# A transformer layer with routed experts: the expert weights are split during attention, rows go to DRAM in long pieces

## The reference, cut to what matters

```
x = layernorm(x + attention(x))
logits = x @ Wg.T;  w, idx = top_k(softmax(logits), 2);  w = w / w.sum()
h = silu(x @ W1[e].T) * (x @ W3[e].T)          # HIDDEN = 352
y = sum over the two experts of w * (h @ W2[e].T)
x = layernorm(x + y)
```

## Time and profile before

| | us |
|---|---|
| three timed runs | 981.38, 982.62, 983.60 (median 982.62) |
| profiled execution, its time | 989.87 |
| its span in the trace | 988.1 |
| attention ends, routing starts | 455.5 |
| routing: VectorE ends | 499.24 |
| experts' stage: first instruction | 499.51 |
| TensorE busy over the span | 799.6 (81%) |
| VectorE, ScalarE, GpSimd busy | 585.2, 480.5, 552.4 |

### The profile page before, as it was taken

How to read it: one execution, slowest core, us unless ns; L and a number is a source line. 1 busy time by engine, 2 the same in 40 slices (tenths; PEclk the granted TensorE clock), 3 DMA queues, 4 the chain that set the end, 5 groups by cost and what they waited for, 6 DMA issues and landing times. The chain is left out here.

```text
span 988.1 us, 22538 instructions
## 1 busy us (share of the span) xinstructions
PE 799.6 (81%) x7657; PEld 598.8 (61%) x7658; DVE 585.2 (59%) x1478; ACT 480.5 (49%) x1150; POOL 552.4 (56%) x719
## 2 busy tenths in 40 slices
PE   5899999999999999982538877888777778787866
PEld 3556666666666666551228776877767777686722
DVE  4678888888888888827935433434434343343445
ACT  1377777777777777755713222222223222222347
POOL 6146666666666666654054666656665656666543
PEclk9899999999999999975668988898998898999979
DMA  5334444434434443204921111111111111112178
GB/s 168 103 122 134 135 135 134 132 131 129 127 127 136 135 135 129 75 8 176 163 46 30 44 41 44 41 41 42 44 43 39 43 42 43 43 42 43 36 238 280
DMA packets 71596, 93.98 MB, mean 95 GB/s; under 512 B 10336, under 2 KB 50016, under 8 KB 71232
## 3 DMA queue, kind: packets, MB, share of 16 engines
q1 hardware_dynamic: 62640, 74.21, 24.1%
q0 software_dynamic: 8704, 17.98, 7.0%
q10 hardware_dynamic: 144, 0.35, 0.1%
HBM read 56.26 MB, written 34.14 MB: 91 GB/s over the span
## 5 line engine op out<-in xcount | busy, mean ns | idle before, releaser
L377 DVE TENSOR_REDUCE neg_max<-ps_s 128x6 f32<-128x768 f32 x256 | 241.1, 952 | 38.7 <-PE ps_s L564 32.7
L242 POOL TENSOR_SCALAR_AFFINE_SELECT probs<-probs 128x512 f32<-128x512 f32 x256 | 162.4, 634 | 164.7 <-ACT probs L314 159.1
L314 ACT ACTIVATE probs<-ps_st 128x768 f32<-128x768 f32 x256 | 207.5, 811 | 81.5 <-PE ps_st L578 80.9
L1122 ACT ACTIVATE act_a<-ps_a 128x352 f32<-128x352 f32 x136 | 63.5, 467 | 310.7 <-DMA dense<-shift_t 160.4
L1103 POOL DMA_INDIRECT picked_rows<-rows_out,pairs x136 | 134.0, 986 | 134.1 <-ACT rows_out L1126 109.9
L1096 POOL DMA_INDIRECT xg<-x_rows,pairs x136 | 131.6, 968 | 79.8 <-issue 40.5
L1160 DVE TENSOR_TENSOR x_low<-ps_xy,x_high 128x128 fp32r<-128x128 f32 x136 | 39.1, 287 | 216.6 <-ACT x_high L1130 173.6
L558 PE MATMUL ps_s<-dense 32*128 32x256 f32 (+1 forms) x1024 | 117.9, 306 | 19.1 <-ACT probs L314 9.3
L1231 PE MATMUL ps_xy<-w_sb,h_t 128*128 (+1 forms) x816 | 129.2, 300 | 1.7 <-ACT rows_out L1126 1.7
L558 PEld LDWEIGHTS ps_s<-dense 32*128 32x128 f32 x1024 | 82.2, 191 | 78.2 <-issue 46.7
L1231 PEld LDWEIGHTS ps_xy<-w_sb,h_t 128*128 128x128 f32 (+1 forms) x816 | 120.6, 213 | 7.1 <-issue 6.8
(11 more groups left out here) (181 smaller groups left out, 1390.6 us busy)
## 6 DMA issues: line engine op xcount, KB each, us to landing
dense_rows<-split SPq DMA_DIRECT2D x32, 512.0 KB, 2.7
dense<-dense_rows SPq DMA_DIRECT2D x64, 256.0 KB
dense<-dense_rows SPq DMA_DIRECT2D x64, 128.0 KB
pick<-picked_rows SPq DMA_DIRECT2D x16, 512.0 KB, 6.0
x_rows<-y_all SPq DMA_DIRECT2D x8, 520.0 KB, 8.1
xt_sb<-xt SPq DMA_DIRECT2D x32, 128.0 KB, 2.2
x_sb<-x SPq DMA_DIRECT2D x32, 128.0 KB, 2.4
out<-normal SPq DMA_DIRECT2D x16, 256.0 KB
```

The source lines that it names most:

```text
L242: last = pool.affine_select(out=part, in_=part, compare_op=ALU.is_ge, fill=0.0, base=0, pattern=[[0, 2 * BLOCKS], [1, P]], channel_multipl ...
L314: act.activation(probs[:, g, 2 * half:2 * half + 2, 0:L + P], ps_st[:, :, 0:L + P], ACT.Exp, scale=float(HEAD_DIM) ** -0.5).then_inc(exp_d ...
L377: v.tensor_reduce(out=neg_max[:, h * GROUP + j:h * GROUP + j + 2, :], in_=ps_s[:, j:j + 2, 0:L + P].rearrange("p b (c t) -> p b c t", t=P) ...
```

## The change

1. Splitting the weights moves from routing into attention. w1 and w3 are taken in 16 pieces of 128x352 (one expert's matrix each) through a ring of four buffers. Four pieces are loaded ahead of the loop and split in the first iteration behind g = 3; one piece is split in each of the batches 0 to 11, behind the work of g = 0. ScalarE copies a piece rounded, VectorE waits for that and subtracts. SyncE loads a later piece at the end of each iteration and w2 in three loads at the end of batches 16 to 18.
2. The DRAM row of token (tile t, place p) becomes p * 64 + t, so that each of the 128 partitions stores eight tiles as one piece of 8 * 520 = 4160 bytes instead of eight pieces of 520. The gathered addresses are computed accordingly (`at_row`), which makes `token` unnecessary.
3. The experts of the 136 tiles are found with two comparisons and a sum over 8 columns on VectorE and two products with the identity on TensorE, instead of a comparison and a reduction over 128x1088.
4. The share block moves to ahead of `place_i`.

```
         for b in range(FIRST, LAST):                                 # ScalarE, attention
...
+                    for c in pieces_at(b, g):
+                        act.wait_ge(piece_landed[c % PIECE_RING], 16 * (c // PIECE_RING + 1))
+                        act.activation(kept["w_high"][:, piece_columns(c)], piece[:, c % PIECE_RING, :], ACT.Copy).then_inc(
+                            piece_high, 1)
...
+                    for c in pieces_at(b, g):                        # VectorE, attention
+                        dve.wait_ge(piece_high, c + 1)
+                        v.tensor_tensor(kept["w_low"][:, piece_columns(c)], piece[:, c % PIECE_RING, :],
+                                        kept["w_high"][:, piece_columns(c)].bitcast(F32), ALU.subtract).then_inc(
+                            piece_low, 1)
...
+        def pieces_at(b, g):
+            if b == FIRST:
+                return range(PIECE_RING) if g == GROUPS - 1 else ()
+            return (b + PIECE_RING,) if g == 0 and 0 <= b < PIECES - PIECE_RING else ()
...
+            def load_piece(c):                                       # SyncE
+                if c >= PIECE_RING:
+                    sp.wait_ge(piece_low, c - PIECE_RING + 1)
+                sp.dma_start(piece[:, c % PIECE_RING, :], (w1, w3)[c // E][:, piece_columns(c % E)]).then_inc(
+                    piece_landed[c % PIECE_RING], 16)
+            for c in range(PIECE_RING):
+                load_piece(c)
...
+                if b == -1:
+                    for c in range(PIECE_RING, 2 * PIECE_RING):
+                        load_piece(c)
+                if 0 <= b < PIECES - 2 * PIECE_RING:
+                    load_piece(b + 2 * PIECE_RING)
+                if W2_AT <= b < W2_AT + len(W2_PARTS):
...
+                    sp.dma_start(kept["w2"][0:m, i * E * D:(i + 1) * E * D], w2[c:c + m, :]).then_inc(w2_landed, 16)
...
-            rows = x1_rows.rearrange("(c t p) d -> c p t d", p=P, t=STORE)
+            rows = x1_rows.rearrange("(p t) d -> p t d", p=P)
...
-                sp.dma_start(rows[c], y_all[:, c * STORE:(c + 1) * STORE, :]).then_inc(x1_stored, 16)
+                sp.dma_start(rows[:, at, :], y_all[:, at, :]).then_inc(x1_stored, 16)
...
+            for i, first in enumerate(sides_at):
+                last = v.tensor_scalar(passed[:, i, :], ends[:], -float(first), consts_at("partition"), ALU.add, ALU.is_le)
+            chain(last)
+            v.tensor_reduce(out=passed_sum[:], in_=passed[:], axis=AX.X, op=ALU.add).then_inc(passed_ready, 1)
...
-            for i in range(2):
-                dve.wait_ge(high_done, i + 1)
-                part = slice(i * WIDE, (i + 1) * WIDE)
-                v.tensor_tensor(w_low[:, part], w_raw[:, part], w_high[:, part].bitcast(F32), ALU.subtract)
-                take(turns - 2 + i)
-            chain(v.tensor_tensor(
-                ge_end[:], consts_at("iota")[:, 0:places].rearrange("p (i o) -> p i o", o=1).to_broadcast([P, places, E]),
-                ends[:].rearrange("p (o e) -> p o e", o=1).to_broadcast([P, places, E]), ALU.is_ge))
-            chain(v.tensor_reduce(out=expert_f[:], in_=ge_end[:], axis=AX.X, op=ALU.add))
-            v.tensor_scalar(expert_of[:], expert_f[:], E - 1.0, None, ALU.min)
+            take(turns - 2)
+            take(turns - 1)
+            dve.wait_ge(experts_listed, 1)
+            v.tensor_scalar(expert_of[0:1, :], ps_total[0:1, 0:places], E - 1.0, None, ALU.min)
...
+                last = mm(ps_total[0:1, first:first + wide], passed_sum[:, i:i + 1], consts_at("ident")[:, 0:wide],
+                          start=True, stop=True)
```

More of the change, by code:

```diff
@@ L47, in attention @@
     FIRST, LAST = -3, n + 2
+    PIECES, PIECE_RING = 2 * E, 4
+    W2_PARTS = range(0, HIDDEN, P)
+    W2_AT = 16
     CHOSEN = 8
@@ L67, in attention @@
         averages = sb("averages", [P, P])
+        piece = sb("piece", [P, PIECE_RING, HIDDEN])
         bias_logits = sb("bias_logits", [P, E])
@@ L124, in attention @@
             sem, ("xb_ready", "y_ready", "stats_ready", "mv_ready", "y_kept"))
+        piece_landed = [sem(f"piece_landed{i}") for i in range(PIECE_RING)]
+        piece_high, piece_low, w2_landed = map(sem, ("piece_high", "piece_low", "w2_landed"))
         CHOICE_STEPS = 9
@@ L656, in _, with routing @@
                     router()
-def routing(nc, consts_at, w1, w3, w2, kept, x1_rows):
+def routing(nc, consts_at, kept, x1_rows):
     y_all, mv_all, choice = kept["y"], kept["mv"], kept["choice"]
@@ L711, in routing @@
         numbers_at, tiles_at = (sb(k, [P, turns, P], BF16) for k in ("numbers_at", "tiles_at"))
-        ge_end = sb("ge_end", [P, places, E])
-        expert_f = sb("expert_f", [P, places])
         second = kept["second"]
[L715 to L719, removed]
+        found, inside, empty, at_row, row = (
+            sb(k, [P, places]) for k in ("found", "inside", "empty", "at_row", "row"))
+        sides_at = range(0, places, P)
+        passed = sb("passed", [P, len(sides_at), E])
+        passed_sum = sb("passed_sum", [P, len(sides_at)])
         ps_behind = ctx.enter_context(nc.psum_tensor("ps_behind", [P, 512], F32))
@@ L928, in _ @@
             chain(v.scalar_tensor_tensor(inside[:], second[:], -float(P), found[:], ALU.mult, ALU.add))
-            chain(v.scalar_tensor_tensor(token[:], ps_keys[:, turns:turns + places], float(P), inside[:], ALU.mult,
-                                         ALU.add))
-            v.tensor_scalar(pairs[:, :, 0], token[:], -1.0, 0.0, ALU.add, ALU.max)
             chain(v.scalar_tensor_tensor(at_row[:], inside[:], float(tiles), ps_keys[:, turns:turns + places], ALU.mult,
                                          ALU.add))
+            v.tensor_scalar(pairs[:, :, 0], at_row[:], -float(tiles), 0.0, ALU.add, ALU.max)
             chain(v.scalar_tensor_tensor(row[:], second[:], float(tokens), at_row[:], ALU.mult, ALU.add))
@@ L951, in _ @@
                    ones[0:1, 0:1], start=True, stop=True).then_inc(keys_turned, 1)
+            pe.wait_ge(passed_ready, 1)
+            for i, first in enumerate(sides_at):
+                wide = min(P, places - first)
+                last = mm(ps_total[0:1, first:first + wide], passed_sum[:, i:i + 1], consts_at("ident")[:, 0:wide],
+                          start=True, stop=True)
+            last.then_inc(experts_listed, 1)
             def spread_out(c):
@@ L1284, in build @@
             "pairs": sb("pairs", [P, places, 2], I32), "expert_of": sb("expert_of", [P, places], I32),
-        }
[L1286 to L1290, removed]
+            "w_high": sb("w_high", [P, 2 * EXPERTS * HIDDEN], F32R),
+            "w_low": sb("w_low", [P, 2 * EXPERTS * HIDDEN], F32R),
+            "w2": sb("w2_sb", [P, -(-HIDDEN // P) * EXPERTS * D]),
+        }
+        attention(nc, x, xt, wqkv, bqk, bv_columns, wo, wo_rows, bo, bo_columns, wg, cst, consts, w1, w3, w2,
+                  kept, dense_rows)
+        routing(nc, consts_at, kept, x1_rows)
         experts_and_combine(nc, consts_at("ident"), consts_at("eps"), kept, x1_rows, picked_rows, out)
```

43 lines of the change are left out of this document (19 added, 24 removed).

## The result

In the first comparison (5 executions of each kernel, in turns) the changed kernel took a median of 978.11 us against 982.62, a ratio of 0.9963, 95% interval 0.9945 to 0.9981: 4.5 us faster. By far the larger part of the measurements says that the change makes no difference that can be told, as the likeliest case of the prediction had it (982.5 against 982.62 before). The first ratio was not seen again, and why it came out so stays open.

The account below looks back on a forecast made before the run. The prediction took TensorE to bound attention and VectorE the routing stage. Its terms, +5.2 + 0.4 - 5.7 = -0.1 us, gave a median of 982.5 us against 982.62, own range 980 to 985.

Parts of the forecast that it names:

- the likeliest case: Whole kernel: the routing stage's gain is paid back in attention; 982.5 us, own range 980 to 985, chance 0.50.
- (b): Attention: the split is hidden because the pipeline takes up 0.43 us a batch; 977.3 us, chance 0.16.
- (f): Experts' stage: it changes by itself, most likely by one 4.9 us wait; 977.6 or 987.4 us, chance 0.10.
- The copies in attention: Attention, 12 batches: a ScalarE copy before the exponential releasing TensorE costs 0.43 us each, +5.2 (4.4 to 5.8).
- VectorE's subtraction: Attention, behind the second row maximum: 0.5 us long, cost put at 0; without cover up to 1.0 us a batch.
- The lead-in: Before the first scores: four piece loads and their split delay router() from 9.07 to 11.5; +0.4 us (0 to 3).
- (d): Lead-in: pieces land later than 10.5 and router() holds the first scores; 985.5 us with 3 us late, chance 0.06.
- Routing: Routing stage: VectorE's chain shortens, the last store sets the end at 493.5; 5.7 us earlier (3.7 to 6.2).
- (e): Routing stage: large pieces don't speed the store, the last lands in 4.7 us, gain 3.7; 984.5 us, chance 0.08.
- The sum: Whole kernel: attention +5.2, lead-in +0.4 and routing -5.7 make -0.1 us; profiled 989.8, median 982.5.
- The experts' stage: Tile loop from 500 us on: only gathered row addresses change, gathers are issued 12 tiles ahead; 0 us.
- My own sign of being wrong: Attention and experts' stage: wrong if the copy takes well under 0.37 us or the experts' stage moves over 3 us.

Follow-up runs that it names:

- the two further ratios: The changed kernel timed again against the kernel before in two further series, no edit: ratios 1.0013 and 0.9996.

## Why the prediction was right, and where its terms were off

The likeliest case held: the routing's gain is paid back in attention and the lead-in. The first comparison's 978.11 alone would not have said so: it lies outside the forecast's own 980 to 985, next to the 977.3 and 977.6 of rivals (b) and (f). What bears the forecast out is the two further ratios and the stages of the traces. By its steps:

- **The copies in attention, +5.2 forecast.** The place and the mechanism were right: the period grew to 12.99 (13.0 forecast), only in the batches with a piece, and moving the copy alone behind that exponential, on top of the subtraction, took all of it back. Rival (b), that it is hidden, is refuted. The mis-sized term is the copy: 0.38, where I took 0.43 from 0.37 to 0.48. The line from the 128-column to the 2816-column copy gave 0.57 as its duration, its row says 0.50; the bound from below, a 352-column row less the queue's overlap, was nearly exact. Eleven periods of 0.385 make 4.2; the twelfth copy, in batch 0, shows no cost (14.6 to 14.7 us to the next copies, 14.5 to 14.8 in the kernel before).
- **VectorE's subtraction, 0.** Right: its row says 0.53 (0.5 forecast), and the maxima behind it run late without holding TensorE; with it at the end of the batch the period did not change.
- **The lead-in, +0.4 forecast.** Wrong in size. The third batch's copies start at 27.34, 26.73 and 27.24 in three profiles with the changed lead-in, and at 25.57, 25.46 and 25.31 with the old one, 1.65 us later on average. Two steps failed. I let the last subtraction start when the last piece had landed, but four of them take 2.71 in a row behind four copies, so `router()` started at 13.15 and not at 11.5. And I put the loads beside the write of `split` at "under a microsecond" for batch 0's rows only, while they lengthened the write itself by 1.0 to 1.3. The first scores came at 18.12, not at 16.8 to 17.3, so rival (d) had its condition met (18 or later), at about half of the 3 us that it allowed.
- **Routing, -5.7 forecast.** Measured 5.5 to 5.7: 44.7 to 39.0 or 39.2. `found` came 6.0 nearer to the stage's start, and the last store sets the end, as forecast. The mark for the stores, under 3 us, was met by the fastest (2.6) but not by the slowest (4.2), and the median is 3.0. Rival (e) is refuted: 520-byte rows in the same place give 3.9 and more, and 1.5 us of stage.
- **The rule on the size of transfers.** The Trainium skill ("DMA: Bandwidth & Descriptors", Specifications) gives line rate from 512 bytes on. The runs don't agree: a store of 520-byte pieces takes 3.9 us at best, one of 4160-byte pieces 2.6, with the same bytes, engine and place. The same page (Anatomy of one DMA) gives 2.0 us plus bytes over 436 GB/s for transfers that GpSimd issues; SyncE issues these stores. The prediction's estimate of 3.2 by that formula lies between the 2.6 at best and the 4.2 at worst, and near the median of 3.0.
- **The sum.** 4.2 + 1.65 - 5.6 = +0.25 us against -0.1 forecast. The last batch's copies, at 399.8 against 394.3 on average of three profiles each, give 5.5 for the first two terms together. The sum is nearer than its terms were, and that was luck: copies 1.0 us too dear and a lead-in 1.25 too cheap cancelled.
- **The experts' stage, 0, with rival (f) for a move of 4.9.** My own sign of being wrong, a move of more than 3 us, was met by the first pair of profiles (8.9), but it was no sign of the change: the tile loop moves by 8 us between profiles of one kernel (439.9 and 431.9; 431.0 and 439.1). I had read one profile and taken its 440 us for the kernel's own. The profiled 978.1 against 988.1 comes nearly all from there. Whether the first comparison's 4.5 us had the same source was not seen, since only one of its executions of each kernel has a profile.

## What to carry to other kernels

Find the instruction in each engine's queue that the bounding engine waits for, and put added work behind it, not in front: the same 12 copies cost 4.2 us ahead of an exponential and nothing one place later, where the engine had a gap of 0.64. In a lead-in, count what the added work does to every engine's queue and to the transfers beside it, since nothing there is hidden by a steady state. And before a difference between two profiled spans is explained, profile the unchanged kernel a second time and compare stage by stage.

## What the runs showed that I had not expected

- What a queued instruction costs less than its row was 0.12 us for a copy of 352 columns (a row of 0.50, a delay of 0.38), where 32 scalings of 128 columns had given 0.09. A term of a sum should be made of such steps in a queue, not of durations.
- The tile loop with its 272 indirect transfers took 430 to 441 us in all fourteen profiles, whose kernels differ there in the gathered addresses and once in the scatter buffers, while the routing stage repeated to 0.2 us for the same code. The mean granted clock in the loop was 0.86 to 0.90 and doesn't sort the profiles by its length. The loop's waits of ScalarE alone ranged from 128 to 184 us, without a clear tie to its length.
- The tail of attention, from the last batch's copies to its end, took 58.5 to 63.8 us in the fourteen profiles, in step with TensorE's mean granted clock there: 58.5 at 0.92, 60.0 to 60.2 at 0.87 to 0.89, 61.3 at 0.86, 62.1 and 62.3 at 0.84 and 0.83, 63.3 to 63.8 at 0.81 and 0.82. Each profile has the clock at 1.00 (2.4 GHz) when the tail begins and at 0.50 (1.2 GHz) for a part of it, about 8 us in the shortest tail and over 20 in the longest. Two profiles of the changed kernel lie near the two ends (58.5 and 63.6), so the change does not set it; what does stays open.
